# An audio encoder layer on one core: one maximum over a pair of banks, and two banks for the scores

## The reference, cut to what matters

```python
scores = jnp.einsum('bhqd,bhkd->bhqk', qp, kp) * scale     # 16 x 8 x 746 x 746
probs = jax.nn.softmax(scores, axis=-1)
attn = jnp.einsum('bhqk,bhkd->bhqd', probs, vp)
```

## Time and profile before

| | |
|---|---|
| Median of 3 runs | 1410.22 us (1408.41 to 1411.82) |
| The profiled execution | 1411.15 us, its span 1409.1 us |
| PE busy | 1259.2 us, 89% of the span |
| DVE busy | 1093.6 us, 78% |
| ACT busy | 968.1 us, 69% |
| POOL busy | 594.4 us, 42% |
| Mean granted clock of TensorE | 0.950 |

### The profile page before, as it was taken

The page is one execution under the profiler, slowest core; times in us unless marked ns, Lnnn a source line. Parts: engine busy times, 40 slices in busy tenths (PEclk is TensorE's granted clock), DMA queues, the critical chain, the costliest instruction groups (busy, mean ns, idle before and its releaser), DMA issues.

```text
span 1409.1 us, 54650 instructions
## 1 busy us (share of the span) xinstructions
PE 1259.2 (89%) x21768; PEld 780.5 (55%) x21768; DVE 1093.6 (78%) x3006; ACT 968.1 (69%) x2479; POOL 594.4 (42%) x544
## 2 busy tenths in 40 slices
PE   6377999999999999999999999999999862999996
PEld 3123546454555555555555455555555431989996
DVE  8368898888888888888888888888889313667775
ACT  5212878787878778787878787877767850667774
POOL 1122424343444536353434344453621222556664
PEclk9558999999999999999999999999999985999999
DMA  7145041423325050404142232505040502333331
GB/s 174 42 57 100 19 84 43 83 66 60 78 48 104 21 120 21 107 36 90 48 78 69 57 82 44 110 15 121 21 107 3 159 24 68 94 88 103 106 104 51
DMA packets 70383, 102.51 MB, mean 73 GB/s; under 512 B 14828, under 2 KB 59875, under 8 KB 69710
## 3 DMA queue, kind: packets, MB, share of 16 engines
q1 hardware_dynamic: 60992, 78.68, 25.2%
q0 software_dynamic: 8416, 20.22, 5.1%
q10 hardware_dynamic: 762, 0.55, 0.1%
HBM read 60.96 MB, written 39.00 MB: 71 GB/s over the span
## 4 chain that ended last, share of the span: by engine, by line
PE 63%; DVE 14%; ACT 11%; issue 5%; DMA 4%; POOL 2%; SPq 1%; another core or an unknown queue 0%; POOLq 0%; ACTq 0%; DVEq 0%
PE psum L977 30%; PE psum L1052 11%; DVE half_max L850 10%; PE psum L982 7%; PE psum L1106 6%; PE psum L1116 6%; ACT arena L605 5%; DMA arena<-in_x_t_dram 2%; ACT q_full L593 1%; ACT k_full L593 1%; DMA k_rows<-k_parts_dram 1%; SPq L399 1%; ACT k_part L593 1%; PE psum L996 1%; PE psum L1097 1%
## 5 line engine op out<-in xcount | busy, mean ns | idle before, releaser
L850 DVE TENSOR_REDUCE half_max<-psum 128x1 f32<-128x373 f32 x1536 | 773.6, 538 | 143.3 <-PE psum L977 134.4
L605 ACT ACTIVATE arena<-psum 128x373 f32<-128x373 f32 (+1 forms) x1536 | 667.3, 487 | 248.6 <-PE psum L977 241.6
L977 PE MATMUL psum<-k_rows,arena 96*32 96x373 bf16 x6144 | 525.5, 332 | 27.4 <-DMA k_rows<-k_parts_dram 15.5
L977 PE MATMUL psum<-arena,k_rows 98*32 98x373 bf16 x6144 | 513.1, 325 | 12.6 <-ACT arena L605 11.6
L1052 PE MATMUL psum<-arena,values 128*32 128x373 f32 (+1 forms) x3072 | 314.0, 476 | 1.5 <-ACT arena L605 1.2
L977 PEld LDWEIGHTS psum<-k_rows,arena 96*32 96x32 bf16 x6144 | 180.2, 97 | 182.6 <-DVE half_max L850 90.4
L977 PEld LDWEIGHTS psum<-arena,k_rows 98*32 98x32 bf16 x6144 | 177.8, 95 | 158.4 <-ACT arena L605 67.5
L503 POOL DMA_INDIRECT routed_rows_dram<-rows,pos_i x96 | 96.2, 1002 | 338.2 <-DVE tok_id L844 247.1
L543 POOL DMA_INDIRECT out_dram<-arena,slot_id x102 | 122.8, 1204 | 88.0 <-issue 52.1
L1052 PEld LDWEIGHTS psum<-arena,values 128*32 128x32 f32 (+1 forms) x3072 | 99.9, 110 | 27.4 <-issue 1.9
L527 POOL TENSOR_TENSOR rstd<-var_eps,minus_half 128x6 f32<-128x6 f32 x16 | 21.5, 1347 | 203.1 <-DVE var_eps L727 203.1
(11 more groups left out here) (155 smaller groups left out, 1442.5 us busy)
## 6 DMA issues: line engine op xcount, KB each, us to landing
arena<-q_parts_dram SPq DMA_DIRECT2D x192, 93.2 KB
k_rows<-k_parts_dram SPq DMA_DIRECT2D x192, 93.2 KB
arena<-routed_rows_dram SPq DMA_DIRECT2D x102, 130.0 KB
q_parts_dram<-q_part SPq DMA_DIRECT2D x16, 559.5 KB, 3.2
k_parts_dram<-k_part SPq DMA_DIRECT2D x16, 559.5 KB, 3.2
arena<-in_x_t_dram SPq DMA_DIRECT2D x3, 703.1 KB, 17.6
seq<-in_w_dram SPq DMA_DIRECT2D x1, 2048.0 KB, 10.3
seq<-in_w_dram SPq DMA_DIRECT2D x8, 256.0 KB, 5.8
```

Of the source, the lines that this page charges most:

```text
L605: nc.scalar.activation(probs[0:kn(kt), G % N_P, j, :], st_bank[s % N_ST][0:kn(kt), 0:HALF], ACT.Exp).then_inc(s_exp, 1)
L850: nc.vector.tensor_reduce(half_max[:, s:s + 1], mx_bank[s % N_MX][:, 0:HALF], AX.X, ALU.max)\
L977: last = nc.tensor.matmul(dst[n:n + m], weights[:, n:n + m], moving, start=start, stop=stop)
```

## The change

The maxima get two pairs of adjoining banks (four banks), and the scores two banks: N_ST and N_MX become 2. TensorE now issues the maximum quads for both halves of a row in every even step, one behind the other into the two banks of a pair, and none in an odd step; there is one wait and one signal for the pair. VectorE reduces the whole row of 746 scores out of both banks with one `tensor_reduce` (over the two inner axes, negated), straight into `neg_max`. The buffer `half_max` and the reduction over it go, and `maxima` is left with two instructions. The counts of the semaphores follow. Which step a fill or a weighing stands behind does not change.

```diff
--- before.py
+++ after.py
@@ -74,7 +74,7 @@
     WEIGH_AT = (7, 11, 15, 19, 23, 27)
     OUT_AT = 4
     SCATTER_AT = (0, 3, 6, 9, 12, 15)
-    N_ST, N_MX, N_P = 3, 3, 3
+    N_ST, N_MX, N_P = 2, 2, 3
     WIDE = 16
     CHUNKS = ((0, 1), (1, 3), (3, 6), (6, 9), (9, 12), (12, B))
     SPAN = B * T - (CONTEXT - 1)
@@ -116,7 +116,6 @@
         merged_t = sb("merged_t", [128, LP])
         xn2_t = merged_t
         rows = sb("rows", [128, NT, ROW])
-        half_max = sb("half_max", [128, STEPS])
         neg_max = sb("neg_max", [128, STEPS // 2])
         max_parts = sb("max_parts", [128, 2, NT, 2, GH], bf16)
         max_rows = [sb(f"max_rows{g}", [2 * GH, L], bf16) for g in range(2)]
@@ -195,7 +194,7 @@
 
         psum = ctx.enter_context(nc.psum_tensor("psum", [128, 8, 512], fp32))
         st_bank = [psum[:, n, :] for n in range(N_ST)]
-        mx_bank = [psum[:, N_ST + n, :] for n in range(N_MX)]
+        mx_pair = [psum[:, N_ST + 2 * n:N_ST + 2 * n + 2, 0:HALF] for n in range(N_MX)]
         o_bank = psum[:, 6, :]
         misc = psum[:, 7, :]
         misc_b = misc.bitcast(bf16)
@@ -729,15 +728,11 @@
 
             def maxima(b, g):
 
-                k = 3 * g
-                dve.wait_ge(s_red, b * STEPS + STEPS // 2 * (g + 1))
-                nc.vector.tensor_reduce(neg_max[:, 24 * g:24 * (g + 1)],
-                                        half_max[:, 48 * g:48 * (g + 1)].rearrange("p (n a) -> p n a", a=2),
-                                        AX.X, ALU.max, negate=True).then_inc(s_max, 1)
-                dve.wait_ge(s_max, b * 6 + (k + 1))
+                k = 2 * g
+                dve.wait_ge(s_red, b * (STEPS // 2) + STEPS // 4 * (g + 1))
                 full = neg_max[:, 24 * g:24 * (g + 1)].rearrange("p (h t) -> p t h", h=GH)
                 nc.vector.tensor_copy(max_parts[:, g, :, 0, :], full).then_inc(s_max, 1)
-                dve.wait_ge(s_max, b * 6 + (k + 2))
+                dve.wait_ge(s_max, b * 4 + (k + 1))
                 nc.vector.tensor_tensor(max_parts[:, g, :, 1, :], full, max_parts[:, g, :, 0, :], ALU.subtract)\
                   .then_inc(s_max, 1)
 
@@ -845,12 +840,13 @@
 
             def body(i, par):
                 for s in range(STEPS):
-                    if live(i, 1):
-                        dve.wait_ge(s_mx, (i + 1) * STEPS + (s + 1))
-                        nc.vector.tensor_reduce(half_max[:, s:s + 1], mx_bank[s % N_MX][:, 0:HALF], AX.X, ALU.max)\
+                    if live(i, 1) and s % 2 == 0:
+                        m = s // 2
+                        dve.wait_ge(s_mx, (i + 1) * (STEPS // 2) + (m + 1))
+                        nc.vector.tensor_reduce(neg_max[:, m:m + 1], mx_pair[m % N_MX], AX.XY, ALU.max, negate=True)\
                           .then_inc(s_red, 1)
-                        if s % 48 == 47:
-                            maxima(i + 1, s // 48)
+                        if m % 24 == 23:
+                            maxima(i + 1, m // 24)
 
                     if s in (12, 16, 20, 26) and live(i, -1):
                         n = (12, 16, 20, 26).index(s)
@@ -991,7 +987,7 @@
                         last = quad(misc[:, D * n:D * (n + 1)], xn_t[:, D * t:D * (t + 1)], wv_sb[:, :])
                 elif name in ("MAX0", "MAX1"):
                     g = int(name[3])
-                    pe.wait_ge(s_max, (i + (1 - g)) * 6 + 3 * (g + 1))
+                    pe.wait_ge(s_max, (i + (1 - g)) * 4 + 2 * (g + 1))
                     for t in range(NT):
                         last = nc.tensor.transpose(misc_b[0:2 * GH, D * t:D * (t + 1)],
                                                    max_parts[:, g, t, :, :].rearrange("p a h -> p (a h)"), identb[:, :])
@@ -1066,14 +1062,17 @@
                         wait(pe, s_exp, scores(i, s) - N_ST)
                         quad(st_bank[s % N_ST][0:kn(kt), 0:HALF], k_rows[par][0:KM, h, D * kt:D * kt + kn(kt)],
                              q_rows[par][0:KM, h, qh * HALF:(qh + 1) * HALF]).then_inc(s_st, 1)
-                    if live(i, 1):
-
-                        b, h, t, half = i + 1, s // 12, s % 12 // 2, s % 2
-                        if s % 48 == 0:
-                            pe.wait_ge(s_ld[s // 48], b * 192 + 192)
-                        wait(pe, s_red, b * STEPS + (s + 1 - N_MX))
-                        quad(mx_bank[s % N_MX][:, 0:HALF], q_rows[1 - par][0:KR, h, D * t:D * (t + 1)],
-                             k_rows[1 - par][0:KR, h, half * HALF:(half + 1) * HALF]).then_inc(s_mx, 1)
+                    if live(i, 1) and s % 2 == 0:
+
+                        b, m = i + 1, s // 2
+                        h, t = m // NT, m % NT
+                        if m % 24 == 0:
+                            pe.wait_ge(s_ld[m // 24], b * 192 + 192)
+                        wait(pe, s_red, b * (STEPS // 2) + (m + 1 - N_MX))
+                        for half in range(2):
+                            last = quad(mx_pair[m % N_MX][:, half, :], q_rows[1 - par][0:KR, h, D * t:D * (t + 1)],
+                                        k_rows[1 - par][0:KR, h, half * HALF:(half + 1) * HALF])
+                        last.then_inc(s_mx, 1)
                     for n, after in enumerate(WEIGH_AT):
 
                         p = (s - after) // PASS
```

## The result

The changed kernel takes 1470.26 us (median of 4 runs, 1469.17 to 1471.24), the kernel before 1411.02 us on the same chip. The ratio is 1.0421 with a 95% interval of 1.0401 to 1.0441: slower by 59 us. The forecast was 1448 us, slower by 37; the direction and the range hold, the size is short by 22 us.

A forecast was written before the change was run, and what follows sets the result against it. TensorE's stream was taken to bound the kernel. A body's terms sum to +2.3 us, +32 over fourteen bodies, plus 5 for the last score body: from 1411.15 to 1448 us, with 8 in 10 at 1409 to 1478.

The forecast's parts named there:

- score ring: With two score banks, third and fourth scores of a group wait for exponentials (round 0.98 us): +4.34 us a body.
- waits at fills that the new waits cover: Fills in the groups at 20, 40, 68 already wait; new waits ahead come out of these: -0.90 us a body.
- late results: Surcharge in a body's first 18 steps, where some TensorE results are seen late: +0.5 us, between 0 and 1.5.
- waits of M quads for VectorE: Seven waits for half_max in a body go with the paired maxima: -1.34 us, between 0 and -1.5.
- MAX1: Fill waiting 1.08 us behind the last maximum; the half_max reduction before it goes: -0.3 us a body, between 0 and -0.5.
- bare group: Four steps without a covering fill: 1.91 us becomes 2.25, third score waiting 0.34; eight groups, 2.72 us a body.
- the four groups with a fill behind step 0: Fills at steps 4, 32, 36, 64 cover the third score; the fourth waits 0.25: 1.00 us a body.
- The maximum ring: A pair's round takes 1.51 of 1.91 us, 0.40 free; the wide reduction takes 0.84 us queued, 0.93 alone.
- The other stages: Last score body +5 us (+3 to +8); stage without scores 0 (-2.5 to +2); first score body 0; rest untouched.
- the faster one: Rival, 15%: relief at VectorE is worth more than the score ring costs; -0.9 us a body, 1401 us.
- A reduction costing twice: Rival, 10%: the reduction over two banks costs two full ones, 1.08 us; about 0.7 us more a body, 1458 us.
- The clock: Rival, 3%: a tenth of the fourteen bodies runs at 1.2 GHz, 78 us more, 1526 us.

The follow-up runs named there:

- x1: The kernel before with two score banks in place of three, nothing else changed: 1444.33 us, ratio 1.0384.
- x7: The changed kernel with exponentials over 238 in place of 373 columns from body 1 on: 1412.17 us, ratio 1.0158.
- x4: The changed kernel with each weighing cut in two halves, standing behind every odd step: 1420.89 us, ratio 1.0215.
- y3: The changed kernel with VectorE's four normalisings one step earlier, ahead of the wide reduction: 1454.76 us, ratio 1.0318.
- x6: The changed kernel with each reduction over only the first 186 columns of each of the two banks: 1418.86 us, ratio 1.0206.
- x8: The changed kernel with GpSimd's six scatters of a body issued one behind the other from step 0: 1445.83 us, ratio 1.0402.
- x3: The kernel before, three and three banks, with both maximum quads behind the even score quad: 1392.62 us, ratio 1.0015.
- y1: The changed kernel as it is, run once more in the third set of experiments: 1473.32 us, ratio 1.0442.
- y2: The kernel before as it is, run once more in the third set of experiments: 1409.48 us, ratio 1.0002.

## Why the prediction was right, and where it was short

The direction, the range and the main mechanism hold. The size is short because terms were left out or too small, in a body (1.2 us of 2.3 too little) and in two of the other stages. For a body, in us:

| Term | Forecast | Measured |
|---|---|---|
| score ring | +4.34 | +4.73 |
| waits at fills that the new waits cover | -0.90 | -0.86 |
| late results | +0.5 | +1.05 |
| waits of M quads for VectorE | -1.34 | -1.36 |
| MAX1 | -0.3 | -0.59 |
| fills behind the normalisings | not in the sum | +0.69 |
| sum | +2.3 | +3.66 (the whole body: +3.50) |

- **The score ring: right in mechanism and nearly in size.** The round of 0.98 us, the 0.34 in a bare group (measured 0.337), the group at step 8 (0.62; measured 0.34 + 0.26) came as forecast. So did the four groups with a fill behind step 0 (0.25; measured 0.28: an exponential without a second wait ahead of it starts 0.385 us behind its quad, where I had read some 0.36). These places give 4.44 (seven bare groups of 0.34, 0.37 at step 82, 0.34 of the 1.08 at step 18, 0.26, four times 0.28). Of the ten groups that I gave no cost, the one with MAX0 waits 0.20, and the one with RANK, which I called nearly covered, 0.09. x1 shows the ring as the cause, x7 and x4 show it from two more sides.
- **The maximum ring: right.** The reduction over two banks takes 0.93 us alone and 0.84 in a queue (the shortest distance of two starts is 0.841), both as estimated. The prediction shows no row for the 0.06 us that a start costs in a queue; 2 x 0.452 - 0.841 gives 0.063. Waits of M quads for VectorE went from 1.36 us a body to none.
- **The waits taken off again: right in sum by luck.** I set 0.90 against the sum, since fills at steps 22, 42 and 70 waited anyway. XNT and XN2T gave 0.28 each. MT gave nothing: it went from 0.61 to 0.66. V at 64 gave 0.16 and HTOK at 4 gave 0.14, which I had not named.
- **The term that was left out: the price of the wide reduction was looked for in its own ring only.** I wrote that 0.40 us is free in the M ring, which holds, and took nothing for the tasks that stand behind a reduction of 0.93 us in VectorE's order. The normalisings hold up bank 7 and with it MT and PROJ: 0.7 us a body more than before, 1.0 with what MT should have given. y3, with the normalisings ahead of the reduction, is shorter by 1.0 us a body; x6 agrees, where my expectation again missed it.
- **MAX1: the gain was twice as large and was lost again.** I forecast -0.3. MAX1's own wait fell from 0.90 to 0.31, and 0.62 came back at the score quad of step 3, whose exponential is seen late. Where nothing is late the gain stays: the first four steps of a body take 2.41 us in x8 and 2.84 in x3, which has three and three banks (both in sets without lateness).

```profile
606.60 0.33 PE L973 MATMUL psum<-arena,k_rows 98*32 98x373 bf16 x4
...
607.07 0.38 PE L992 MATMUL psum<-identb,max_parts 128*8 128x128 bf16 x4
...
607.82 0.85 ACT L604 ACTIVATE arena<-psum 128x373 f32<-128x373 f32 x2 [0.78 <-PE psum L973]
...
608.35 0.10 PEld L973 LDWEIGHTS psum<-arena,k_rows 98*32 98x32 bf16 x4 [0.69 <-ACT arena L604]
608.36 0.34 PE L973 MATMUL psum<-arena,k_rows 98*32 98x373 bf16 x4 [0.31 <-ACT arena L604]
```

  In the changed kernel the score quad of step 1 starts at 606.60. Its exponential is the first of the two at 607.82, 1.22 later, and step 3 waits for it until 608.36. In x6 it comes after 0.38 us.
- **The surcharge for late results: half of what it was.** I took +0.5, within 0 to 1.5. At step 18 the wait is 1.08, of which 0.34 is the bare group's, so 0.74 where step 19 had 0.62 before. But the score at step 3 waits 0.62 and that at step 7 0.59 (0.28 of it the ring's) for late exponentials too, places that I did not name: 0.12 + 0.62 + 0.31 = 1.05.

```profile
618.83 0.34 PE L973 MATMUL psum<-arena,k_rows 98*32 98x373 bf16 x4
...
620.05 0.85 ACT L604 ACTIVATE arena<-psum 128x373 f32<-128x373 f32 x2 [1.73 <-PE psum L973]
...
620.59 0.34 PE L973 MATMUL psum<-arena,k_rows 98*32 98x373 bf16 x4 [0.93 <-ACT arena L604]
```

  This answers to the earlier trace rows: the score at 618.83, its exponential at 620.05, the score two steps on at 620.59. The same place in x1, in a set without lateness, reads:

```profile
610.07 0.34 PE L977 MATMUL psum<-arena,k_rows 98*32 98x373 bf16 x4
...
610.52 0.85 ACT L605 ACTIVATE arena<-psum 128x373 f32<-128x373 f32 x2 [1.12 <-PE psum L977]
...
611.06 0.34 PE L977 MATMUL psum<-arena,k_rows 98*32 98x373 bf16 x4 [0.16 <-ACT arena L605]
```

  0.45 us from score to exponential, and 0.99 to the score two steps on.
- **The other stages: under-sized by 9 us, with gains of 5 that I did not expect.** I gave body 0 nothing, for its fills are few. Few fills mean more bare groups, and it lost 5.1 us. How much of that is the ring is open: in y1 and y2 the same two kernels have 66.8 and 64.7 us there, a loss of 2.1, at a mean granted clock of 0.92 and 0.90 in place of 0.93 and 0.94; x1 has 67.5 against 64.7 of x3 in the same set, 2.9. The last body lost 8.7 where I had 5, beyond the 8 of its range. The stage without scores gained 2.7, where I had 0 within -2.5 to +2 (0.5 in y1 and y2). The 2.7 gained behind the last score, which I called untouched, are not explained.
- In all, a body gave 3.5 in place of 2.3 (14 bodies: +17 us), body 0 5 us and the last 3.7 more, less 2.7 at the start and 2.7 behind the last score: +20 of the 22 that were missing.
- **The rivals.** Of the faster one nothing was seen: relief at VectorE did come, and was worth 2 us a body at most. A reduction costing twice fell (0.93 us). The clock stayed at full in all middle bodies and in the last body with scores; in body 0 the mean is 0.93 and was 0.94 (the 0.98 of the earlier trace rows is of a window that begins 4.3 us later). What the Trainium skill (Perfetto Trace Analysis, Optimization Strategy) says of consistent bubbles and too few buffers is borne out by x1, for the scores.

## What to carry to other kernels

A ring of N banks is long enough if N times the shortest distance between two uses covers the round (start of the matmul to start of the reader, reader, release), worked out for the actual order of the stream: here 0.98 us against 0.64 with two banks and 0.96 with three, where the 0.02 that lack show in no wait. Where banks can't be had, spreading a long piece of work (the weighing) evenly between the uses took the waits out of the bare groups (x4). And when short instructions are merged into a long one, look at what stands behind it in that engine's queue and who waits for that: moving four small tasks ahead of it was worth 1.2%.

## What was not expected of the hardware

- The kernel before takes 1411 and 1409 us in two of the four sets and 1391 and 1390 in the other two, at the same granted clock in the middle bodies. In the first two, exponentials start up to 1.8 us behind their quad in place of 0.38 to 0.45, and reductions up to 1.6 in place of 0.39, mostly in the first 18 steps of a body, where GpSimd's scatters run; in the other two this is not seen, with the same program parts. In the trace of the kernel before, a scatter runs between the quad and the exponential in 44 of the 48 places where ScalarE stood idle over 0.15 us and the exponential came over 0.6 us behind, and in 27 of the 397 where it came sooner. In the changed kernel it is 47 of 53 and 20 of 363. In x3, in a set without lateness, a scatter runs there 41 times and none of these exponentials is late. So the scatters go with the lateness, but do not bring it alone. It is not the chip number: 13 is on a set of each kind. Whether that number names one and the same chip, whether the scatters cause it, and what else must come with them, is open: the one run that moved the scatters fell in a set without lateness.
- A `tensor_reduce` over 746 fp32 values in two adjoining banks takes 0.93 us alone and 0.84 in a queue, where one over 373 takes 0.54 and 0.45: per value it is the same, and only the start is saved.
